# Where a row of the scan copies its input, which engine sends the expert transfers, and one more leading step: a recurrent two-layer kernel on one core

## Time and profile before

| | |
|---|---|
| median of 3 runs | 1483.17 us (1479.82 to 1483.81) |
| profiled execution | 1483.56 us, its span 1481.8 us |
| busy in the span | VectorE 1267.5 us (86%), TensorE 982.6 (66%), ScalarE 706.7 (48%), GpSimd 692.2 (47%) |
| DMA | 141.23 MB, mean 95 GB/s |
| layer 0: chunk steps | 169.6 to 797.9 us on VectorE |
| layer 1: rows of the scan | 880.0 to 1440 us on VectorE |

### The profile page before, as it was taken

How to read it: one execution, slowest core, us unless ns; L and a number is a source line. 1 busy time by engine, 2 the same in 40 slices (tenths; PEclk the granted TensorE clock), 3 DMA queues, 4 the chain that set the end, 5 groups by cost and what they waited for, 6 DMA issues and landing times. The chain is left out here.

```text
span 1481.8 us, 15782 instructions
## 1 busy us (share of the span) xinstructions
PE 982.6 (66%) x3548; PEld 573.3 (39%) x3549; DVE 1267.5 (86%) x2435; ACT 706.7 (48%) x1337; POOL 692.2 (47%) x630
## 2 busy tenths in 40 slices
PE   3670125877878787777534675379888898987531
PEld 1140123555555555555324521134434444443200
DVE  5768986999999999999998888399989898899944
ACT  2542212555555455555322263068678576784305
POOL 5003772222222222222110037639888898888770
PEclk9875556889898889988757588579999999999955
DMA  9993111000000000000522133145454453544741
GB/s 369 220 185 54 36 47 25 21 20 21 21 21 18 20 20 20 19 18 11 144 85 57 29 121 124 57 144 163 155 185 167 153 188 125 187 139 151 162 51 57
DMA packets 94436, 141.23 MB, mean 95 GB/s; under 512 B 22068, under 2 KB 66881, under 8 KB 89905
## 3 DMA queue, kind: packets, MB, share of 16 engines
q1 hardware_dynamic: 83696, 118.01, 26.8%
q0 software_dynamic: 10688, 22.67, 5.7%
HBM read 108.02 MB, written 34.74 MB: 96 GB/s over the span
## 5 line engine op out<-in xcount | busy, mean ns | idle before, releaser
L1919 DVE TENSOR_TENSOR ps<-ps,cv 128x512 f32<-128x512 f32 x256 | 162.9, 682 | 27.3 <-ACT ps L1451 27.3
L1034 PE MATMUL ps<-Q,ident 128*128 128x512 f32 x256 | 143.7, 654 | 49.4 <-issue 24.8
L757 POOL TENSOR_TENSOR Q<-LR,xn 128x512 f32<-128x512 f32 x96 | 122.1, 1272 | 57.5 <-DVE LR L1928 42.2
L723 POOL DMA_INDIRECT y_tok<-xnT,meta x72 | 75.5, 1049 | 151.4 <-ACT xnT L1204 143.4
L700 POOL DMA_INDIRECT slots_x<-xn,sl_put x64 | 74.6, 1165 | 130.2 <-DVE sl_put L1575 111.1
L873 PE MATMUL ps<-wd_a,xn 128*128 x576 | 99.5, 325 | 36.7 <-ACT xn L1198 36.7
L497 POOL TENSOR_TENSOR x<-x 128x512 f32<-128x512 f32 x28 | 32.9, 1175 | 188.1 <-DVE x L1721 188.1
L738 POOL DMA_INDIRECT slots_x<-xn,sl_put x64 | 65.0, 1015 | 103.4 <-DVE sl_put L1588 84.2
L883 PE MATMUL ps<-x,ident 128*128 128x64 f32 x512 | 72.3, 293 | 58.7 <-issue 46.4
L856 PE MATMUL ps<-wg_a,xnT 128*128 x144 | 97.2, 763 | 11.3 <-issue 10.0
L873 PEld LDWEIGHTS ps<-wd_a,xn 128*128 128x128 f32 x576 | 83.8, 224 | 50.5 <-issue 49.0
(11 more groups left out here) (337 smaller groups left out, 2813.2 us busy)
## 6 DMA issues: line engine op xcount, KB each, us to landing
cv<-bc_scr SPq DMA_DIRECT2D x64, 512.0 KB
xn<-bc_scr SPq DMA_DIRECT2D x28, 1024.0 KB
qkv_scr<-cv SPq DMA_DIRECT2D x24, 256.0 KB, 6.0
slots_x<-O POOLq DMA_DIRECT2D x18, 260.0 KB, 8.8
xnT<-slots_x SPq DMA_DIRECT2D x72, 64.0 KB, 1.8
x<-in_x SPq DMA_DIRECT2D x8, 512.0 KB, 6.0
O<-bc_scr SPq DMA_DIRECT2D x4, 1024.0 KB
wu_a<-in_w_e SPq DMA_DIRECT2D x12, 256.0 KB, 4.0
```

Of the source, the lines that this page charges most:

```text
L723: pool.indirect_dma_start(out=y_tok, out_offset=bass.IndirectOffsetOnAxis(ap=meta_bits[:, n, 0:1], axis=0), in_=yg[:, k, :], in_offset=Non ...
L757: pool.tensor_tensor(yc_g0[:, n % 4, :], st_g0[:, n % 2, :], cn, ALU.mult).then_inc(yc_ready, 1)
L1034: pe.matmul(ps[:, 4, :], ident[:], yc_g0[:, n % 4, :], start=(n == 0), stop=(n == NS - 1)).then_inc(y0_used, 1)
L1919: tt(dBu(g), ps[:, 2 + g, :], b_rows[:, n % 4, :], ALU.mult).then_inc((inject0, b_used)[g], 1)
```

## The change

Seven edits.

1. `FIRST` goes from 3 to 4: four leading steps without tiles, 24 with tiles, three plain ones before the last. `gates` of the first six groups moves on VectorE from the end of the last plain step to behind the last step. `attention_out` of these groups moves on TensorE from ahead of the last step to behind it and behind `o_mean(1, 0)`.
2. GpSimd in row 0: 48 of the 64 scatters, then `delta_sum` and `delta_h` for row 1, then the other 16 scatters.
3. SyncE waits for the scatters and loads the first two experts in row 1 at n = 4, not in row 0 at n = 13. For this the C rows of row 1 stay in the buffer O (`c_rows`), and the copied output of row 0 goes to `wproj`.
4. Pieces: row 1 has them from n = 6 on (10, before 19), rows 2 and 3 have 21, rows 4 to 6 have 20 (before: 19 in rows 1 to 4, 18 in rows 5 and 6). The states with two pieces are other ones.
5. The store of an expert and the loads of the expert after next are issued by ScalarE right behind the 14th piece (before: by SyncE one state later).
6. At n = 15 ScalarE does `dh_copy` ahead of `taps1` and the pieces (before: behind them).
7. VectorE's `finish` moves from n = 1 to n = 2.

The core of the diff:

```diff
-FIRST = 3
+FIRST = 4
...
-            return c_later if c else c_first
+            return c_later if c > 1 else c_first
...
-            twice = (2, 11, 13) if c <= 4 else (11, 13)
-            q = (c - 1) * 19 - max(c - 5, 0) + n + sum(m < n for m in twice)
+            if c == 1:
+                return (n - ROW1_START,) if n >= ROW1_START else ()
+            twice = (2, 6, 9, 10, 11) if c <= 3 else (2, 6, 9, 11)
+            q = NS - ROW1_START + (c - 2) * 20 + min(c - 2, 2) + n + sum(m < n for m in twice)
...
+                    if n == 4 and c == 1:
+                        first_experts()
...
             for i in range(NT):
+                if i == 3 * NT // 4:
+                    for g in range(GD):
+                        delta_sum(1, 1, g)
+                    for g in range(GD):
+                        delta_h(1, 1, g)
...
-            for g in range(GD):
-                delta_sum(1, 1, g)
-            for g in range(GD):
-                delta_h(1, 1, g)
...
+            step(NCH - 1, False)
+            o_mean(1, 0)
             for g in range(6):
                 attention_out(g)
-            step(NCH - 1, False)
-            o_mean(1, 0)
...
+                if p == PIECES - 1:
+                    act.wait_ge(moe_out, q + 1)
+                    act.dma_start(slots_y1[e * CAP:(e + 1) * CAP, :].rearrange("(i p) c -> p i c", p=P), yg1).then_inc(y1_stored, 16)
+                    if e + 2 < E:
+                        for dst, src in expert_parts(e + 2):
+                            act.dma_start(dst, src).then_inc(e1_loaded[e % 2], 16)
...
+                    if c < LAST and n == NS - 1:
+                        for g in range(GD):
+                            dh_copy(r, t, g)
...
-                if c < LAST:
-                    for g in range(GD):
-                        dh_copy(r, t, g)
...
-            step(AFTER + 3, False, late=lambda: gates(range(6)))
             step(NCH - 1, False, last=True)
+            gates(range(6))
...
-                    if n == 1 and c:
+                    if n == 2 and c:
                         finish(c - 1, t)
```

More of the change, by code:

```diff
@@ L300, in dA, with s1_of @@
             return (dA_near, dA_far)[k // 4 % 2][:, k % 4, :]
-        s1 = O[:].rearrange("p e t -> p (e t)")
+        s1_later = O[:].rearrange("p e t -> p (e t)")
+        def s1_of(c):
+            return s1_later[:, c * L:(c + 1) * L] if c else wproj[:]
         x_loaded = sem("x_loaded")
@@ L433, in build @@
         PIECES = 14
+        ROW1_START = 6
         NCU = 3 * B
@@ L478, in piece_units, with expert_parts @@
                 return ()
[L479 to L480 removed]
+            if c == 1:
+                return (n - ROW1_START,) if n >= ROW1_START else ()
+            twice = (2, 6, 9, 10, 11) if c <= 3 else (2, 6, 9, 11)
+            q = NS - ROW1_START + (c - 2) * 20 + min(c - 2, 2) + n + sum(m < n for m in twice)
             return (q, q + 1) if n in twice else (q,)
+        def expert_parts(e):
+            k = e % 2
+            return ((w_e1[k], d["w_e1"][e * P:(e + 1) * P, :]), (flat(w_e2[k]), d["w_e2"][:, e * FC * D:(e + 1) * FC * D]),
+                    (xg1[k], slots_x1[e * CAP:(e + 1) * CAP, :].rearrange("(i p) c -> p i c", p=P)))
         def in_bank(r, g):
@@ L583, in _, with first_experts @@
             turn(1)
-            def expert_loads(e, k):
-                sp.dma_start(w_e1[k], d["w_e1"][bass.ds(e * P, P), :]).then_inc(e1_loaded[k], 16)
-                sp.dma_start(flat(w_e2[k]), d["w_e2"][:, bass.ds(e * FC * D, FC * D)]).then_inc(e1_loaded[k], 16)
-                sp.dma_start(xg1[k], slots_x1[bass.ds(e * CAP, CAP), :].rearrange("(i p) c -> p i c", p=P)).then_inc(e1_loaded[k], 16)
-            def expert_store(e):
-                sp.wait_ge(moe_out, e * PIECES + PIECES)
-                sp.dma_start(slots_y1[bass.ds(e * CAP, CAP), :].rearrange("(i p) c -> p i c", p=P), yg1).then_inc(y1_stored, 16)
+            def first_experts():
+                sp.wait_ge(scattered1, 16 * 2 * NT)
+                for e in range(2):
+                    for dst, src in expert_parts(e):
+                        sp.dma_start(dst, src).then_inc(e1_loaded[e], 16)
             def bc_store(r):
@@ L633, in row @@
                     if n == 13 and c < LAST:
-                        if c == 0:
-                            sp.wait_ge(scattered1, 16 * 2 * NT)
-                            for k in range(2):
-                                expert_loads(k, k)
                         c_load(c + 1, 0)
@@ L640, in row @@
                         b_load(c + 1, 0)
-                    for q in (piece_units(c, n - 1) if n else piece_units(c - 1, NS - 1) if c else ()):
-                        e, p = divmod(q, PIECES)
-                        if p == PIECES - 1:
-                            expert_store(e)
-                            if e + 2 < E:
-                                expert_loads(e + 2, e % 2)
             bc_store(0)
@@ L731, in _ @@
                     y_scatter(c)
-            pool.wait_ge(slots_ready, 2)
-            pool.wait_ge(xn_ready, 2 * NT)
-            for i in range(NT):
-                for j in range(2):
-                    pool.indirect_dma_start(out=slots_x1, out_offset=bass.IndirectOffsetOnAxis(ap=sl_put[:, j, i:i + 1], axis=0),
-                                            in_=xn[:, i, :], in_offset=None, bounds_check=E * CAP - 1,
-                                            oob_is_err=False).then_inc(scattered1, 16)
             def delta_sum(r, s, g):
@@ L748, in delta_h @@
                 pool.tensor_tensor(dh1[s][:, g, :], del1[s][:, g, :], h1[s][:, g, :], ALU.mult).then_inc(dh_made, 1)
+            pool.wait_ge(slots_ready, 2)
+            pool.wait_ge(xn_ready, 2 * NT)
+            for i in range(NT):
+                if i == 3 * NT // 4:
[3 more added lines that the diff above has]
+                        delta_h(1, 1, g)
+                for j in range(2):
+                    pool.indirect_dma_start(out=slots_x1, out_offset=bass.IndirectOffsetOnAxis(ap=sl_put[:, j, i:i + 1], axis=0),
+                                            in_=xn[:, i, :], in_offset=None, bounds_check=E * CAP - 1,
+                                            oob_is_err=False).then_inc(scattered1, 16)
             def row(c, s):
@@ L1300, in _ @@
             step(AFTER + 2, False, early=decay_rates, late=lambda: oT_scale(range(6)))
-            step(AFTER + 3, False)
             step(NCH - 1, False, last=True)
@@ L1973, in _ @@
                     dve.wait_ge(mix_silu, G4 + k)
-                    o.link(tt(v, v, s1[:, last * 512:(last + 1) * 512], ALU.mult))
+                    o.link(tt(v, v, s1_of(last), ALU.mult))
                     tt(xs, xs, v, ALU.add).then_inc(out_ready, 1)
```

2 lines of the change are left out of this document (1 added, 1 removed).

## The result

The changed kernel took 1476.62 us (median of 20 runs, 1464.91 to 1482.91), the kernel before 1480.55 us in as many. The ratio is 0.9964, with a 95% interval of 0.9949 to 0.9979: faster by 0.36%, where 1453 us was forecast. The profiled execution took 1475.68 us with a span of 1473.9. It begins row 0 of layer 1 at 859.77 (before 879.98), row 1 at 951.58 (before 988.92), row 7 at 1330.12 (before 1350.73). So 37.3 us had been won when row 1 began; rows 1 to 6 gave back 16.7, and row 7 with the tail 12.7.

What follows compares the result with a forecast made beforehand. VectorE, busy 86% of the span, was taken as the bound, with its waits to be removed: 1483.56 - 16.5 - 17.4 + 4.1 = 1453.8, forecast as 1453 us. Range 1444 to 1463 for this case alone, 1425 to 1473 at about 0.8.

Steps and rivals of the forecast that it cites:

- part 3: Layer 1, rows 1 to 6: piece table, earlier copy, later finish and ScalarE's issues together +4.1 us, bounds -26 and +15.
- the end: From the first gather on: 123.6 us, set by GpSimd's 64 gathers, nothing in it changes; 0.
- Part 1: Layer 0: step 2's wait for the transposed tile goes and gates and products move; -16.5 us, bounds -20 and -12.
- +3.0 for the variance: Layer 0's end: 48 TensorE products, hidden before, stand between mean and variance, so VectorE gets the variance 3.0 us later.
- Part 2: Layer 1, row 0: the pause after 48 scatters lets late signals through; -17.4 us, bounds -20 and 0.
- rival B: Row 0: signals stay held through the pause in the scatters, so its stalls remain; 1471 us, chance 0.12.
- ScalarE's 26 issues: Rows 1 to 6: 11 to 13 us of ScalarE, a third of it costing time; +3.4 us, bounds 0 and 11.
- Rival C: Rows 1 to 6: ScalarE's issues cost 1.5 us each, each delaying the next piece; 1489 us, chance 0.05.
- The piece table: Rows 1 to 6: row 1 falls to VectorE's 56.0 (-3.5), seven more pieces in rows 2 to 5 +6.9, row 6 +1.
- The copy first: Rows' ends: earlier copy gives VectorE 3.7 us, but the TensorE-ScalarE chain needs 62 us a row, so once only; -3.7.
- rival A: Rows 1 to 6 are bound by order, not TensorE; every row goes at 55.97 us; 1423 us, chance 0.17.
- D: Layer 0: VectorE holds up the last nine scatters, ending them 30 us later; 1483 us, chance 0.03.

Runs made afterwards that it cites:

- e5: The changed kernel again, unedited, on a chip with late signals; 1480.37 us, ratio 0.9939.
- e14: The changed kernel, unedited, on the same chip as e13; 1480.50 us, ratio 0.9898.
- e4: The changed kernel with SyncE again issuing the experts' store and loads one state later; 1412.01 us, ratio 0.9787.
- e18: e17 with ScalarE again issuing the experts' stores and loads, same chip; 1448.44 us, ratio 0.9729.
- e17: e16 with the scatters of row 0 cut after 32 in place of 48; 1426.39 us, ratio 0.9595.
- e2: The changed kernel with finish back at n = 1; 1415.03 us, ratio 0.9806.
- e6: The changed kernel with the experts' transfers issued by SyncE again and finish back at n = 1; 1459.29 us, ratio 0.982.
- e12: The kernel before with dh_copy ahead of taps1 and pieces, and the changed kernel's piece table; 1441.84 us, ratio 1.001.
- e7: The kernel before with only dh_copy moved ahead of taps1 and pieces; 1474.06 us, ratio 0.9908.
- e8: The changed kernel with dh_copy back behind taps1 and pieces; 1485.42 us, ratio 0.9988.
- e13: The kernel before, unedited, traced on the same chip as e14; 1489.13 us, ratio 0.9979 against itself.
- e1: The kernel before with only four leading steps and the first gates and attention_out behind the last step; 1420.71 us, ratio 0.9856.
- e16: e15 with two pauses in row 7's 64 gathers, GpSimd waiting for VectorE behind 24 and behind 48; 1425.80 us, ratio 0.9561.
- e15: e6 with e3's piece table; 1453.97 us, ratio 0.9749.
- e3: The changed kernel with six pieces moved back into row 1 (16 there, 19 in rows 2 to 5, 20 in row 6); 1430.55 us, ratio 0.9929.
- e10: The kernel before with only the layer 0 reordering of e1 and the earlier dh_copy of e7; 1410.11 us, ratio 0.9783.
- e9: e6 with two pauses in row 7's 64 gathers, behind 24 and behind 48; 1411.64 us, ratio 0.9783.
- e11: e10 with the two gather pauses of e9; 1411.94 us, ratio 0.9785.

## Why the prediction was wrong

The direction was right, the size not: -30 us forecast, -3.9 measured in the 20 runs (-10.6 in e5 and -12.3 in e14, against the kernel before on their chips). In the profiled pair parts 1 and 2 gave 3.4 us more than forecast, part 3 missed by 12.6 and the end by 12.7. Two steps failed: in part 3 the path of the rows ("the chain TensorE-ScalarE needs its 62 us whatever VectorE does", and only a third of ScalarE's issues on it), and at the end the claim that GpSimd's gathers set it.

**Part 1, -16.5: right in sum, wrong in one term.** From step 0 to row 0 the traces have 710.4 and 692.3 us (-18.1), and 706.8 and 691.4 on one chip (-15.3). Step 3 shows no wait at line 1725. But the +3.0 for the variance did not come: it reached VectorE 0.3 us earlier after the mean's start than before. The 3.52 us that TensorE had waited for ScalarE between mean and variance took in most of the products, and products and variance ran at the higher clock (5.5 and 1.95 us in place of 6.5 and 3.5).

**Part 2, -17.4: right.** Row 0 -17.1 and -15.3. The pause did let the signals through: TensorE started again at 920.6, 6.4 us after the 48th scatter, so rival B fell. GpSimd came 2.3 us late into row 1, which cost VectorE 1.1.

**Part 3, +4.1: wrong by 11 to 13 us.** Its terms, by the runs that took each alone:

- ScalarE's 26 issues: +3.4 forecast, with 11 as the upper bound. Measured 13.6 (e4 against the changed kernel), 13.2 (e18 against e17), and 7.5 (e2 against e6). I had set their length against ScalarE's idle time. But each group stands just behind a piece, where TensorE comes next to wait. Rival C had the mechanism right and the price of an issue wrong: about 0.5 us, not 1.5. The 1.61 of the earlier trace rows ends a train of issues without a pause, in which the last six took 1.37 to 1.61 each; that a queue was full is not shown.
- The piece table: +4.4 forecast (-3.5 + 6.9 + 1), measured +12.7 (e12 against e7). The -3.5 was counted for the table, yet edit 6 alone takes the same 3.5 us off row 1 with its 19 pieces. And I priced the pieces at a mean of 0.74, which is about what one frees in row 1 (0.68). The nine that moved into rows 2 to 6 made TensorE busy 11.8 us longer there, 1.3 a piece; row 6, which I kept near its 56 us, took 60 to 61.
- The copy first: -3.7 forecast, measured -10.9 (e7) and 8.0 when undone (e8). Here the error went the other way: the chain did not need 62 us by itself, and rival A, that the order binds the rows, had a part of the truth.
- The late finish: 0 forecast, 7 us beside ScalarE's issues (e2), 1 without them (e6 against e4).

Added up: -10.9 + 12.7 + 14.8 (edits 5 and 7 together, e6 against e5) is +16.6, against +16.7 and +14.9 measured. The runs form one path from the kernel before by e7, e12 and e6 to e5, so they must add up but for the step from e12 to e6, which brings in edits 1 to 3 and makes 0.4 us. What the sum shows is that these three cost the rows nothing. How large each term is depends on where in the path it is taken, as 10.9 and 8.0 for the copy show.

**The end, 0: wrong.** +6.6 us on one chip (e14 against e13), +12.7 in the first pair. The step that failed is that gathers set the end and nothing in it changes. From the first gather to the end it took 139.3 us where 123.6 was forecast; on one chip it took 132.0 before (e13) and 143.0 after (e14), and 99.1 in e1. What sets it where signals are late is VectorE's row 7, held by them under the gathers: 106 and 112 us, against 73.4 in e16. In e16 and in e1 the end follows the last gather by 14.5 and 14.4 us, so there the gathers do set it; in e14 it comes 61 us behind. Why the changed kernel loses 6 us more is settled in part at most. With the early `finish` row 7 and tail took 143.6 us (e6) in place of 148.5 (e5), and 142.2 (e15, another table too) in place of 147.1 (e14); before they took 140.5 (e13). So the late `finish` may account for some 5 us, but two executions of the kernel before differ by 9.4 there. The gathers of the changed kernel also start 4 us after the row in place of 8.5, which no run takes by itself.

Rivals A and D did not come as a whole. Rows 2 to 5 took 63 to 69 us, not 56. The last scatters of layer 0, now beside a working VectorE, came every 1.43 us (nine intervals from 213.93 to 226.79 us, the last scatter below), which is the 1.44 forecast. The prediction's estimate by the Trainium skill, "SBUF — State Buffer", section "SBUF: two separate sides", had 3.1 us for each, and that did not come. Slow ones had been two before, not one: 4.34 and 4.89 us, both beside VectorE operations of 4.42 us.

```profile
226.79 0.97 POOL L704 DMA_INDIRECT slots_x<-xn,sl_put  x1 [0.30 <-issue]
```

The version with edits 1 to 3 and 6, e3's table and the pauses (e16) beats both kernels: 0.9561 on a chip with late signals; on the other kind I did not run it. On the other kind e10, with edits 1 and 6 alone, has 0.9783. No table that took pieces out of row 1 beat the old one in the rows (349.8 us in e10, 358.3 in e15), and e10 with the pauses was never run on a chip with late signals.

## What to carry to other kernels

Where two engines hand one buffer back and forth, their queues are one chain: an instruction put behind a hand-over can cost up to its full length, however idle the engine is on average. Here 14 us of issues cost 7.5 to 13.6. Before you unload a stretch, ask which engine bounds it once the other edits are in; work taken from a stretch that is no longer bound by it saves nothing and still costs where it lands. Where signals come late under a long row of indirect DMAs, try a short pause in it; where they did not (e9, e11), the pauses changed nothing.

## What the runs showed of the hardware

- On some chips signals between engines come late under a long burst of GpSimd's indirect DMAs. Bursts of 64 (83 us) stalled VectorE for 33 us in row 0 (e13) and 33 in row 7; a burst of 32 (42 us) left it idle for 1.0 us of row 0 (e17). One pause of 6.3 us was enough in row 7 (e16). Why signals are late is not shown.
- It went with the chip: the kernel before took 1441 us on two and 1491 to 1493 on three, with row 7 at 74 (e1, where edit 1 leaves row 7 alone) or 106 us (e13). Each chip was seen in one series only.
- TensorE runs slower after it has waited. In e3 a pair of products of 0.81 us took 1.43 behind a wait of 4.6 us; the granted clock was 1.00 (2.4 GHz) from 962.0 to 967.5 us and 0.50 (1.2 GHz) from 973.2 to 977.0, behind the wait.
